# Layer 0's routed experts: weights of the later tiles copied on GpSimd from a resident block, slots laid out by partition, and another order of VectorE's work

## The reference, cut to what matters

```
# cond of layer 0, for each token
chosen = top2(sigmoid(router logits) + bias)        # 2 of 8
gate   = sigmoid scores of the chosen, normed
c = shared(x) + sum over chosen e of gate[e] * (gelu(x @ r_w1[e].T) @ r_w2[e].T)
# ffn of layer 0
probs = softmax(c @ gate_w)                          # 8 experts
top_p, top_idx = top_k(probs transposed, 8)          # each expert takes 8 of 32 tokens
xin = take_along_axis(c, top_idx)
y = (gelu(xin @ w1, exact) @ w2) * top_p
x = x + zeros.at[top_idx].add(y)
```

## Time and profile before

| | us |
|---|---|
| median of 3 runs | 560.34 |
| lowest and highest | 558.55, 560.71 |
| the profiled execution's own time | 560.55 |
| its span | 559.2 |
| TensorE busy | 526.6 |
| VectorE busy | 435.0 |
| ScalarE busy | 358.9 |
| GpSimd busy | 181.8 |

### The profile page before, as it was taken

The page is one execution under the profiler, slowest core; times in us unless marked ns, Lnnn a source line. Parts: engine busy times, 40 slices in busy tenths (PEclk is TensorE's granted clock), DMA queues, the critical chain, the costliest instruction groups (busy, mean ns, idle before and its releaser), DMA issues.

```text
span 559.2 us, 10400 instructions
## 1 busy us (share of the span) xinstructions
PE 526.6 (94%) x3320; PEld 452.9 (81%) x3320; DVE 435.0 (78%) x1135; ACT 358.9 (64%) x814; POOL 181.8 (33%) x188
## 2 busy tenths in 40 slices
PE   8999999999976998989999989899999999999997
PEld 7877886777766887978989977788999999997785
DVE  4987668467654589797876458998999999999966
ACT  4567753474534556355443346898888888888965
POOL 4688785773000577890730000001100000000100
PEclk9999999999999999989999999999999999999999
DMA  8635943343898422301200000113111111112111
GB/s 283 190 151 222 358 155 103 76 182 81 253 307 242 137 50 57 102 0 39 98 1 1 1 1 0 21 26 33 21 21 19 21 30 29 30 30 56 39 57 39
DMA packets 50405, 49.83 MB, mean 89 GB/s; under 512 B 23264, under 2 KB 42752, under 8 KB 49792
## 3 DMA queue, kind: packets, MB, share of 16 engines
q1 hardware_dynamic: 48304, 44.84, 26.9%
q0 software_dynamic: 2048, 4.33, 2.6%
HBM read 37.87 MB, written 10.69 MB: 87 GB/s over the span
## 4 chain that ended last, share of the span: by engine, by line
PE 63%; DVE 15%; SPq 8%; issue 5%; POOL 3%; DMA 3%; ACT 3%; DVEq 0%; ACTq 0%
PE bank L1718 6%; PE bank L370 5%; PE bank L372 5%; PE bank L371 5%; PE bank L2157 4%; PE bank L2243 4%; PE bank L2147 4%; SPq L888 3%; PE bank L2184 3%; PE bank L2185 3%; POOL y_rows L1025 3%; SPq L856 2%; DMA w_ring<-routed_w 2%; PE bank L1788 2%; DVE scat L1843 2%
## 5 line engine op out<-in xcount | busy, mean ns | idle before, releaser
L2538 POOL CAST h_high<-h 128x256 fp32r<-128x256 f32 x15 | 6.4, 425 | 197.7 <-ACT h L2349 191.3
L1025 POOL DMA_INDIRECT y_rows<-routed_y,slot_at x32 | 32.5, 1017 | 64.0 <-DMA routed_y<-y_out 54.6
L370 PE MATMUL bank<-xin_high,sw_high 128*128 128x256 f32 x128 | 43.8, 343 | 4.0 <-DVE sw_low L1691 3.5
L2184 PE MATMUL bank<-taps_high,q1T 128*128 128x512 f32 x94 | 43.1, 459 | 1.0 <-ACT q1T L2312 0.6
L846 POOL DMA_INDIRECT routed_x<-x_rows,slot_at x32 | 31.9, 996 | 17.2 <-issue 11.5
L2185 PE MATMUL bank<-taps_low,q1T 128*128 128x512 f32 x94 | 37.1, 394 | 0.0
L2147 PE MATMUL bank<-x,lstm_wx 128*128 128x128 f32 x256 | 34.4, 277 | 1.7 <-ACT gates_t L2285 0.9
L371 PE MATMUL bank<-xin_low,sw_high 128*128 128x256 f32 x128 | 36.0, 281 | 0.0
L2285 ACT ACTIVATE gates_t<-bank,lstm_b_half 128x128 f32<-128x128 f32 x96 | 28.3, 365 | 12.1 <-PE bank L2157 8.7
L372 PE MATMUL bank<-xin_high,sw_low 128*128 128x256 f32 x128 | 35.9, 281 | 0.0
L2147 PEld LDWEIGHTS bank<-x,lstm_wx 128*128 128x128 f32 x256 | 32.0, 191 | 4.5 <-ACT gates_t L2285 3.3
(11 more groups left out here) (325 smaller groups left out, 1757.2 us busy)
## 6 DMA issues: line engine op xcount, KB each, us to landing
big<-gates_scratch SPq DMA_DIRECT2D x3, 2048.0 KB, 7.5
w_ring<-routed_w SPq DMA_DIRECT2D x39, 132.0 KB, 3.1
w<-in_f_w SPq DMA_DIRECT2D x16, 256.0 KB, 4.5
onehot<-topi_scratch SPq DMA_DIRECT2D x8, 512.0 KB, 4.8
routed_y<-y_out SPq DMA_DIRECT2D x13, 204.0 KB, 3.6
xs<-routed_x SPq DMA_DIRECT2D x13, 192.0 KB, 3.6
outT<-x SPq DMA_DIRECT2D x15, 128.0 KB, 2.0
xT<-in_xT SPq DMA_DIRECT2D x3, 512.0 KB, 7.4
```

Source lines behind the costliest of these rows:

```text
L370: pe.matmul(dst, wh[:, cols], vh[:, :], start=start, stop=False)
L1025: pool.indirect_dma_start(y_rows[c % 2][:, r, i, :], None, ys_dram[:, :], bass.IndirectOffsetOnAxis(slot_at[:, r, tile:tile + 1], 0)).then ...
L2184: pe.matmul(dst, q, taps_high[:, 2 - j, :], start=True, stop=False)
```

## The change

1. Only the first 15 tiles' weights (FIRST_TILES) still come by DMA with a register. For the other 24, all eight experts' weights are loaded once into SBUF as `w_resident` (8 x 132 KB), over buffers that the shared experts have used, so that the load waits for the last shared product. GpSimd reads the 24 expert numbers into its own registers and copies each tile's weights from `w_resident` into the ring, in front of the gather.
2. A slot s = 128 * tile + row is now kept at row * 39 + tile of `routed_x` and `routed_y`: three tiles of a partition are one run of 1536 or 1632 bytes instead of three of 512 or 544. VectorE has four more small instructions for it.
3. SyncE issues the loads for the one-hots, the raw weights and the slots between the trios. `weight_sums` goes from trio 5 to trio 6.
4. In groups 0 and 1 `combine` goes from ahead of the copies of experts 4 and 6 to behind those of 5 and 6, the `scat` instructions to experts 2, 4 and 7, and the transpose and tables of the choice from the group's end to the first expert of the next.

```diff
@@ slots_placed
-                dve.tensor_copy(slot_at[:, :, :], pair_at).then_inc(s_sided, 1)
+                dve_pos(dve.tensor_scalar(tile_of, pair_at, 0.5 - P / 2, 1.0 / P, ALU.add, ALU.mult))
+                dve_pos(dve.tensor_scalar(tile_of, tile_of, MAGIC, None, ALU.add))
+                dve_pos(dve.tensor_scalar(tile_of, tile_of, MAGIC, float(1 - SPARSE_TILES * P), ALU.subtract, ALU.mult))
+                dve_pos(dve.scalar_tensor_tensor(row_of, pair_at, float(SPARSE_TILES), tile_of, ALU.mult, ALU.add))
+                dve.tensor_copy(slot_at[:, :, :], row_of).then_inc(s_sided, 1)
@@ new, called at the head of gather_pool
+            w_resident = over(at_wres, "w_resident", 0, E * W_SPARSE).rearrange("p (e k) -> p e k", e=E)
+            FIRST_TILES = RING * TRIO
+            def later_experts():
+                pool.wait_ge(s_sided, EXPERTS_READY)
+                for k in range(FIRST_TILES, SPARSE_TILES):
+                    copied_experts.append(pool.value_load(tile_expert[0:1, k:k + 1], min_val=0, max_val=E - 1))
+            def copy_weights():
+                pool.wait_ge(s_wcat, 48)
+                for k in range(FIRST_TILES, SPARSE_TILES):
+                    m = k // TRIO
+                    if k % TRIO == 0:
+                        pool.wait_ge(s_sd, m - RING + 1)
+                    w = w_resident[:, ds(copied_experts[k - FIRST_TILES], 1), :].rearrange("p o k -> p (o k)")
+                    pool.tensor_copy(w_ring[k % FIRST_TILES], w).then_inc(s_trio[m % RING], 1)
@@ load_xs; store_y likewise
-                rows = xs_dram[m * TRIO * P:(m + 1) * TRIO * P, :].rearrange("(j p) c -> p j c", j=TRIO)
+                rows = xs_dram.rearrange("(p k) c -> p k c", k=SPARSE_TILES)[:, m * TRIO:(m + 1) * TRIO, :]
@@ shared_sp
-                for k in range(SPARSE_TILES):
+                for k in range(FIRST_TILES):
                     tile_experts.append(sp.value_load(tile_expert[0:1, k:k + 1], min_val=0, max_val=E - 1))
                 for m in range(RING):
                     load_weights(m)
-                choice_store(0)
@@ sparse_sp
                 for m in range(RING):
                     load_xs(m)
+                choice_store(0)
+                sp.wait_ge(s_down, ALL_UNITS)
+                sp.dma_start(w_resident, wcat.rearrange("e p k -> p e k")).then_inc(s_wcat, 16)
                 sp.wait_ge(s_vc, 32)
-                for k in range(2):
-                    gather_loads(0, k)
-                load_slots(0)
-                load_raw_weights()
                 for m in range(TRIOS):
                     if m + RING < TRIOS:
                         load_xs(m + RING)
-                        load_weights(m + RING)
+                    if m < 2:
+                        gather_loads(0, m)
+                    if m == 3:
+                        load_raw_weights()
+                    if m == 4:
+                        load_slots(0)
                     store_y(m)
@@ sparse_turn
-                pe.wait_ge(s_trio[m % RING], TRIO_LOADED * (m // RING + 1))
+                pe.wait_ge(s_trio[m % RING], TRIO_LOADED + TRIO_COPIED * (m // RING))
@@ group_pe
-                    if g in (1, 2) and u == 0:
+                    if g in (1, 2) and u == 4:
                         pe.wait_ge(s_dc, g * TABLES + TURNED)
+                    if g in (1, 2) and u == 2:
+                        pe.wait_ge(s_ye, g * E + 1)
+                        choice_transpose(g, y_bank[0][:, SIDE])
                     expert_down(w)
...
-                    if g < 2 and u == U2 - 1:
-                        pe.wait_ge(s_ye, g * E + E - 1)
-                        choice_transpose(g + 1, y_bank[0][:, SIDE])
@@ group_dve
-                    if g < 2 and e in (4, 6):
-                        combine(DENSE + 2 * g + e // 2 - 2)
-                    if g < 2 and e == 6:
-                        choice_scores(g + 1)
-                    if g < 2 and e == 7:
-                        choice_probs(g + 1)
...
+                    if g < 2:
+                        if e in (2, 4):
+                            scatter_tables(g, range(8) if e == 2 else range(8, 12))
...
                     output_copy(g, e)
...
-                if g < 2:
-                    choice_tables(g + 1, y_bank[0][:, SIDE])
-                    choice_rows(g + 1)
+                    if g < 2:
+                        if e in (5, 6):
+                            combine(DENSE + 2 * g + e - 5)
+                        if e == 6:
+                            choice_scores(g + 1)
+                        if e == 7:
+                            scatter_tables(g, range(12, 16))
+                            choice_probs(g + 1)
+                    if 1 <= g < 3 and e == 0:
+                        choice_tables(g, y_bank[0][:, SIDE])
+                        choice_rows(g)
```

More of the change, by code:

```diff
@@ L628, in build_program @@
             pair_at = in_x1("pair_at", 680, 2 * HALF)[:, :].rearrange("p (r i) -> p r i", r=2)
+            tile_of, row_of = (in_x1(n, 712 + 2 * HALF * k, 2 * HALF)[:, :].rearrange("p (r i) -> p r i", r=2)
+                               for k, n in enumerate(("tile_of", "row_of")))
             past = in_x1("past", 712, SPARSE_TILES * (E - 1))[:, :].rearrange("p (k e) -> p k e", e=E - 1)
@@ L847, in scatter_pool @@
                                                 x_rows[:, i * C:(i + 1) * C], None).then_inc(s_scat, 16)
-            tile_experts = []
+            w_resident = over(at_wres, "w_resident", 0, E * W_SPARSE).rearrange("p (e k) -> p e k", e=E)
+            FIRST_TILES = RING * TRIO
+            tile_experts, copied_experts = [], []
+            def later_experts():
[10 more added lines that the diff above has]
+                    pool.tensor_copy(w_ring[k % FIRST_TILES], w).then_inc(s_trio[m % RING], 1)
             def load_weights(m):
-                if m >= RING:
-                    sp.wait_ge(s_sd, m - RING + 1)
                 for k in range(TRIO * m, TRIO * (m + 1)):
-                    sp.dma_start(w_ring[k % (RING * TRIO)], wcat[ds(tile_experts[k], 1), :, :].rearrange("o p k -> (o p) k")
+                    sp.dma_start(w_ring[k], wcat[ds(tile_experts[k], 1), :, :].rearrange("o p k -> (o p) k")
                                  ).then_inc(s_trio[m % RING], 16)
@@ L862, in load_xs @@
                     sp.wait_ge(s_xt, m - RING + 1)
-                rows = xs_dram[m * TRIO * P:(m + 1) * TRIO * P, :].rearrange("(j p) c -> p j c", j=TRIO)
+                rows = xs_dram.rearrange("(p k) c -> p k c", k=SPARSE_TILES)[:, m * TRIO:(m + 1) * TRIO, :]
                 sp.dma_start(xs[m % RING].rearrange("p (j c) -> p j c", j=TRIO), rows).then_inc(s_trio[m % RING], 16)
-            TRIO_LOADED = 16 * (TRIO + 1)
+            TRIO_LOADED, TRIO_COPIED = 16 * (TRIO + 1), 16 + TRIO
             def store_y(m):
                 sp.wait_ge(s_yv, m + 1)
-                rows = ys_dram[m * TRIO * P:(m + 1) * TRIO * P, :].rearrange("(j p) c -> p j c", j=TRIO)
+                rows = ys_dram.rearrange("(p k) c -> p k c", k=SPARSE_TILES)[:, m * TRIO:(m + 1) * TRIO, :]
                 sp.dma_start(rows, y_out[m % 2].rearrange("p (j c) -> p j c", j=TRIO)).then_inc(s_yst[m % 2], 16)
@@ L923, in sparse_up @@
                 for j in range(TRIO):
-                    w = w_ring[(TRIO * m + j) % (RING * TRIO)]
+                    w = w_ring[(TRIO * m + j) % FIRST_TILES]
                     mm = pe.matmul(bank[4 + m % 2][:, j * P:(j + 1) * P], w[:, 0:P], x_cols[m % 2][:, j * P:(j + 1) * P],
@@ L1017, in gather_pool @@
             def gather_pool():
+                later_experts()
+                copy_weights()
                 y_stored(pool, TRIOS - 1)
@@ L1954, in group_dve @@
                             gather_onehot(g + 1, (e - 2) // 2 if g == 0 else e - 3)
-                    if g == 2:
+                    if g < 2:
+                        if e in (2, 4):
+                            scatter_tables(g, range(8) if e == 2 else range(8, 12))
+                    elif g == 2:
                         if e == 7:
                             scatter_tables(g, range(8, 16))
-                    else:
-                        tables_at = 2 if g == GROUPS - 1 else 4
-                        if tables_at <= e < tables_at + 4:
-                            scatter_tables(g, range(4 * (e - tables_at), 4 * (e - tables_at + 1)))
+                    elif 2 <= e < 6:
+                        scatter_tables(g, range(4 * (e - 2), 4 * (e - 1)))
                     if k + 3 < GROUPS * E and not (g and e == 1):
```

3 lines of the change are left out of this document (2 added, 1 removed).

## The result

| | before | after |
|---|---|---|
| median of 13 runs each, us | 560.82 | 557.86 |
| lowest and highest, us | 558.55, 562.84 | 556.18, 560.39 |
| ratio to before, with its 95% interval | | 0.9948 [0.9933, 0.9963] |
| the profiled execution, and its span, us | 560.55, 559.2 | 558.08, 556.8 |
| granted TensorE clock over the span | 0.997 | 0.988 |

The forecast was 550.4. The direction was right, clear of the noise by the interval, and the time is inside the range, at its upper end, but over two thirds of the gain are missing. The stages show where. First the windows of the changed kernel by stage, with the same columns and cut at the same places of the program as the earlier trace rows: the trios, then groups 0, 1 and 2. Groups 1 and 2 begin where their first unit's second weights begin, so a wait ahead of these counts to the group before. The windows are of the one execution that was profiled.

The account below looks back on a forecast made before the run. TensorE was taken to set the pace, so only its idle time could be won. From 560.55 us, 5.6 for the trios and 4.5 for groups 0 and 1 were subtracted, giving 550.4; range 544.5 to 558.

Parts of the forecast that it names:

- the groups' term: Expert groups 0 and 1: VectorE's new order lets slots_turn come earlier, 4.5 us gained for both, bounds 0 and 8.3.
- the trios' term: Routed trios: with GpSimd's copies as the pace, the experts' first product comes at 178.5 instead of 184.15, 5.6 us earlier.
- term c: Trios: GpSimd's time per tile for a weight copy plus its register step, taken as 0.7 us, bounds 0.44 and 1.27.
- the formula 155.1 + 24c + 6.6: End of the trios: resident block ready, 24 copies at c each, then last trio's turn to experts' first product; 178.5.
- the best case: Trios: copies cost nothing and TensorE's own 28.0 us remain, 8.6 us earlier; whole kernel 546, chance 0.15.
- the factor 1.27: GpSimd's copies: slowdown from VectorE working beside them, read from line 285's 1272 to 1622 ns; made a copy 0.56 us.
- The resident block: Start of the trios: the 1056 KB load issued at 147.5 takes 7.5 us, ready at 155.1; bounds 3.1 and 9.6.
- The reads of expert numbers: GpSimd before the trios: 24 reads from 133.0 at 0.58 us each end at 147, hidden by the shared experts.
- The half way house: Trios: expert-number reads at 1.26 us or c near 0.95 eat part of the gain; 558.5, chance 0.10.
- VectorE's new order gives nothing: Groups: combines take as long and TensorE waits elsewhere for as much, only the trios gain; 555, chance 0.12.
- GpSimd is the bound: Trios: GpSimd's copies eat both gains from c = 1.12 us on; 564.1 at the upper bound, chance 0.08.
- DMA stays the bound: Trios: DMA engines still set the pace, 27.5 us for some 7.1 MB against TensorE's 28.0; no chance given.

Follow-up runs that it names:

- e1: The changed kernel with choice_exp on ScalarE moved from a group's end to behind the gelu of the next group's third unit: 550.67 us, ratio 0.9823.
- e5: The changed kernel with the slots again in the order of the kernel before (part 2 undone): 559.16 us, ratio 0.9971.
- e4: The changed kernel with all 39 tiles' weights again by SyncE's DMAs (part 1 undone), no resident block or GpSimd copies: 565.23 us, ratio 1.0075.
- e2: The changed kernel with the expert groups' order of the kernel before (part 4 undone): 554.0 us, ratio 0.9885.
- e8: e1 with slots_turn(g-1, 1) one unit later on TensorE and the combines behind the copies of experts 4 and 6: 546.81 us, ratio 0.9746.

## Why the prediction was wrong, and where it was right

**The step that failed is the one of the groups, 4.5 us of gain.** It was worked out on VectorE's queue and TensorE's, and its end was "`slots_turn(0, 1)` follows at 218.0 where it was 220.65". VectorE's part was exact (33.3 us after the first product, for 33.35). That TensorE could follow was wrong. The scores' later place was in the same schedule, behind the second combine, and the working did not ask who reads them: ScalarE, whose exponential stands ahead of the next group's gelus. ScalarE was busy for only 21.1 of 35.5 us in the earlier trace rows, and its queue was not listed. The measured size: 4.8 us lost in place of 4.5 gained between the experts' first product and layer 1, and 8.1 between the changed kernel and e1 in the same stretch (146.6 less 138.5).

With that one instruction moved, e1 gains 3.3 us in the experts on the kernel before (7.2 in the median on the changed one), and its 550.67 is next to the forecast's 550.4. That nearness is luck, two errors of opposite sign: against e1 the groups' term was 1.2 too large (4.5 for 3.3), and the trios' term 1.1 too small (184.15 less e1's 177.43 is 6.7, for 5.6). The 4.5 was itself 5.9 less 1.4 taken off for GpSimd's work beside VectorE. At the turn of group 1's last expert e1 was 5.1 us ahead (70.1 for 75.2), and lost 1.8 of it again behind that point.

**The trios, forecast 5.6, measured 6.5 in the stage** and 7.4 by the two points 184.15 and 176.76 that the sum used; 0.9 of this is the earlier start, which other kernels show without the change. That the stage gets shorter once the weights leave SyncE's queue was right; that the copies would then set its pace was not, because term c was mis-sized. A copy took 407 ns, for an assumed 560 with contention, and its register step 46 ns, for the 147 taken over from SyncE's row; the first nine copies in 3.85 us are 0.43 each and the next six in 3.13 are 0.52, where c was 0.7. At that rhythm the copies no longer set the pace, so the formula 155.1 + 24c + 6.6 didn't apply, and TensorE's own work did: 30.1 us with its waits, where the best case had 28.0. The rate of 0.40 us for 264 columns that the Trainium skill's "GPSIMD Engine Reference", section "3.1 Elementwise — side-by-side cycle accounting", gives an estimate for agrees with the 407 ns measured; the factor 1.27, taken from a two-input line beside it, did not carry over to the one-input copy, except for single ones up to 921 ns. Nor does show what the forecast read in it: VectorE was at work beside all three executions of line 285, and the shortest, 1272 ns from 272.1 on, ran beside a two-input instruction of VectorE (272.19 to 273.90).

**The resident block**, forecast ready at 155.1: issued at 146.85, its first reader started at 152.33, 5.5 us later for 1056 KB. The value taken was 7.5. It had the same effect as a smaller c: the copies began nearly 3 us sooner than forecast, and the wait of 1 to 2 us before the turn of trio 5 (154.58) did not come.

```profile
146.85 0.39 SPq L922 DMA_DIRECT2D w_resident<-routed_w  x1
```

**The reads of expert numbers** on GpSimd were a hit in pace: 24 in 12.9 us between first and last start, 0.56 each for the 0.58 taken. They did not wait for the scatter's issue to end, as the forecast had it (133.0): the first stands at 129.3, the last scatter at 132.23. They were done before the block came, and no wait ended with them.

```profile
L864 POOLq TENSOR_LOAD <-tile_expert x24: 282/286/496, 129.3 to 142.2; - x24
```

**The layout of the slots**, costed at nothing but what it gave to the stores: 1.3 us by e5's medians, with nothing not excluded. **Moving `weight_sums` and the loads**, costed at nothing: within the 0.6 us between e4's trios and those of before. SyncE's new order was not tried by itself.

**The rivals.** The half way house (558.5, with 0.10) came nearest by its time, by luck: its mechanism, reads at 1.26 us or c near 0.95, is refuted by 0.56 and 0.43. "VectorE's new order gives nothing" (555, with 0.12) named VectorE's fullness; against e2 the order is worth 3.3 us in e1 and 7.2 in e8, with two more moves, when nothing stands behind it. "GpSimd is the bound" is refuted by its waits for TensorE. "DMA stays the bound" is refuted for the changed kernel, where only 1.4 us of TensorE's waits in the trios end with a DMA. With the weights by DMA it is not refuted: e4's waits stand where its DMA engines are full. That an order change could lose time by ScalarE was not among the rivals, so the chance of 0.07 for slower held nothing of the true mechanism.

**The clock.** The forecast counted the low clock of group 1 as something to win back. It got worse: after each 4 us of TensorE standing still, the next products ran at half the pace (four in 2.08 us for 1.02), and the granted clock of the two groups behind was 0.92. As 1.00 is 2.4 GHz, part of that time was at 1.2 GHz. By the sums under e1 this is about 3.3 of the 7.6 us. e1's groups 0 and 1 have 1.00; its group 2, which has the 2.60 us wait near its start, has 0.95.

## What to carry to other kernels

When an instruction is made later in program order, list who reads its result and what stands behind each reader on the reader's own engine, also on an engine that is idle two fifths of the time: an in-order queue passes the delay on to work that has nothing to do with it. Move the reader along with the writer (here one exponential, 7.2 us), and check that what the reader feeds may come later too; the same move in the kernel before cost 9.4 us. Where one wait stops the main engine for some 4 us, count the slower pace behind it as well (here 3.3 us beside 4.3). And read a DMA share in slices around the waits, not over the stage.

## What the runs showed of the hardware

- A GpSimd copy of 128x264 float32 whose source address comes from a register took 407 ns (402 at best), with 46 ns for the register step, while VectorE was busy 18.7 of the stage's 30.1 us. A read of a number from SBUF into a GpSimd register took 286 ns and its step 147; the rhythm was 0.56 us.
- A table load of ScalarE stands directly behind the instruction before it and ahead of the wait: at 202.01, behind a gelu that ended at 202.00, for an exponential that started at 209.01. It is off the path when the wait is long; the one back to the gelu (210.24 to 211.52) is on it. It took 1.28 us, and the next ACTIVATE started 0.02 us behind it. The Trainium skill, "ScalarE: Activation LUTs", section "What ACT_TABLE_LOAD costs", adds a drain of about 1.38 us to a switch; these rows show no such gap, neither ahead of the load nor behind it.
- With the weights by DMA, a lower mean DMA share over the stage did not mean a shorter wait: 0.86 with 6.6 us of waits for weights before, 0.75 with 7.9 in e4. The 20 us with e4's waits had 1.04 and 0.97 in their two halves. With 15 such loads and one of 1056 KB no wait ended with weights, though the share was 1.03 from 152 to 156 us there too.
